# Graph layer on one Trainium2 core: masks made by GpSimd and turned by DMA, lower sums behind the projection, late one-hots at full width in two buffers

## The reference

```python
h    = max(layernorm(x), 0)                       # per node, over 128 features
idx  = the first 25 neighbours of each row of adj # in the order of their numbers
agg  = max over those of h[idx]                   # and with 0 where a row has <= 25 neighbours
out  = x + relu(concat([h, agg]) @ W + b)
```

## Time and profile before

| what | us |
|---|---|
| median of 3 runs | 698.95 (697.47 to 699.57) |
| the profiled execution | 697.45, its span 695.7 |
| PE busy in the span | 630.9 (91%) |
| DVE busy | 613.7 (88%) |
| ScalarE busy | 472.3 (68%) |
| POOL busy | 50.3 (7%) |
| DVE maxima of the picks (224) and of the late rounds (84) | 270.5 and 102.4 |
| ScalarE: masks (56) and copies of turned masks (64) | 57.4 and 62.2 |

### The profile page before, as it was taken

The page is one execution under the profiler, slowest core; times in us unless marked ns, Lnnn a source line. Parts: engine busy times, 40 slices in busy tenths (PEclk is TensorE's granted clock), DMA queues, the critical chain, the costliest instruction groups (busy, mean ns, idle before and its releaser), DMA issues.

```text
span 695.7 us, 10819 instructions
## 1 busy us (share of the span) xinstructions
PE 630.9 (91%) x3376; PEld 297.4 (43%) x3376; DVE 613.7 (88%) x813; ACT 472.3 (68%) x642; POOL 50.3 (7%) x41
## 2 busy tenths in 40 slices
PE   2479998999989999899999999899999999999976
PEld 2133443535445354443545344353535335353423
DVE  3368999899998999989998899989998899988997
ACT  2689478783777639775795947777497927959120
POOL 1300021000210002100030002100021000300000
PEclk9899999999999999999999999999999999999999
DMA  9520141510415103251303313151122411020100
GB/s 361 199 87 27 60 152 68 182 70 16 152 73 200 60 15 136 83 188 60 128 23 122 151 60 151 68 196 57 41 122 87 185 60 32 16 107 1 60 15 16
DMA packets 19127, 67.64 MB, mean 97 GB/s; under 512 B 4499, under 2 KB 7830, under 8 KB 16534
## 3 DMA queue, kind: packets, MB, share of 16 engines
q1 hardware_dynamic: 19094, 67.26, 25.7%
HBM read 42.08 MB, written 4.19 MB: 67 GB/s over the span
## 4 chain that ended last, share of the span: by engine, by line
PE 66%; DVE 16%; issue 10%; ACT 4%; DVEq 1%; DMA 1%; POOL 1%; ACTq 0%
PE picked L506 18%; PE picked L507 17%; PE ring L455 14%; DVE late_hot L684 4%; PE side L469 4%; PE ring L449 4%; DVE hot L659 4%; PE side L463 4%; DVE best L775 3%; DVE best L678 3%; PE final L534 2%; PE final L538 2%; PE final L491 1%; DMA adj_in<-in_adj_dram 1%; DVEq L771 1%
## 5 line engine op out<-in xcount | busy, mean ns | idle before, releaser
L678 DVE TENSOR_TENSOR best<-picked,best 128x1024 f32<-128x1024 f32 x224 | 270.5, 1218 | 38.2 <-PE picked L507 36.0
L506 PE MATMUL picked<-hot,h_hi 128*128 128x512 f16 x512 | 194.5, 380 | 15.0 <-DVE best L775 7.5
L507 PE MATMUL picked<-hot,h_lo 128*128 128x512 f16 x512 | 194.0, 379 | 0.0
L506 PE MATMUL picked<-late_hot,hi_skew 128*128 128x512 f16 x336 | 127.6, 380 | 13.1 <-DVE late_hot L684 8.2
L507 PE MATMUL picked<-late_hot,lo_skew 128*128 128x512 f16 x336 | 127.3, 379 | 0.0
L344 ACT ACTIVATE late_rank<-ring,late_bias 128x512 bf16<-128x512 f32 x128 | 81.4, 690 | 57.6 <-PE ring L455 57.6
L775 DVE TENSOR_TENSOR best<-picked,best 128x1024 f32<-128x1024 f32 x84 | 102.4, 1219 | 8.3 <-PE picked L507 8.2
L378 ACT COPY best<-picked 128x1024 f32<-128x1024 f32 x32 | 32.2, 1013 | 102.6 <-PE picked L507 102.6
L659 DVE TENSOR_SCALAR hot<-rank 128x4096 f16<-128x4096 bf16 x64 | 89.4, 1399 | 12.0 <-ACT rank L344 12.0
L349 ACT ACTIVATE past<-side,bias_cut 128x512 bf16<-128x512 f32 x128 | 88.3, 690 | 6.2 <-PE side L469 4.9
L344 ACT ACTIVATE rank<-ring,bias_big 128x512 bf16<-128x512 f32 x128 | 83.1, 692 | 5.2 <-PE ring L455 4.9
(11 more groups left out here) (76 smaller groups left out, 562.1 us busy)
## 6 DMA issues: line engine op xcount, KB each, us to landing
adj_in<-in_adj_dram SPq DMA_DIRECT2D x16, 2048.0 KB, 7.7
late_skew<-late SPq DMA_DIRECT2D x32, 192.0 KB, 2.3
x_in<-in_x_dram SPq DMA_DIRECT2D x8, 512.0 KB, 8.5
xres<-in_x_dram SPq DMA_DIRECT2D x16, 256.0 KB, 7.8
late_skew<-late SPq DMA_DIRECT2D x16, 256.0 KB, 2.4
late_skew<-late SPq DMA_DIRECT2D x32, 128.0 KB, 2.0
out_dram<-xres SPq DMA_DIRECT2D x16, 256.0 KB, 2.0
late_skew<-late SPq DMA_DIRECT2D x32, 64.0 KB, 1.9
```

Source lines behind the costliest of these rows:

```text
L506: nc.tensor.matmul(dst, hi[:, slot, k, :], onehot, start=start, stop=False)
L507: return nc.tensor.matmul(dst, lo[:, slot, k, :], onehot, start=False, stop=stop)
L678: nc.vector.tensor_tensor(best[:, half, s, :, :], picked[s][:, :, :], best[:, half, s, :, :], ALU.max).then_inc(picked_read, 1)
```

## The change

- Masks: in the prologue DVE makes group 0's from four separate loads of its adjacency, after the features' statistics; all others are made by POOL, from a strided view, into a layout ordered by class. SP turns each quarter with a transposing DMA into one of two buffers `mask_t[:, slot]`. ScalarE's masks and copies and PE's transposes are gone, and with them four of the twenty ring entries a step.
- The features are loaded ahead of the adjacency.
- The lower sums of g+2 stand at the end of step g, behind the projection; before, those of g+1 stood after use 4.
- Late ranks are spread over uses 4 to 9 (5 to 8 before), prefixes over 4 to 11 (5 to 12), ranks over 9 to 14 (9 to 13); the count follows use 11, not 9.
- Late one-hots are made at full width, into two of now four buffers of `hot`, in turn. The first is made after use 12.

```diff
-    LATE_WITH, PREFIX_WITH, RANK_WITH = spread_over(5, 8), spread_over(5, 12), spread_over(9, 13)
-    LATE_HOT_USES, COUNT_USE, MASK_USES = (10, 11), 9, (4, 9)
+    LATE_WITH, PREFIX_WITH, RANK_WITH = spread_over(4, 9), spread_over(4, 11), spread_over(9, 14)
+    LATE_HOT_USE, COUNT_USE = 12, 11
...
-        mask_t = sb("mask_t", [P, K, ROWS], BF16)
+        mask_t = sb("mask_t", [P, 2, K, ROWS], BF16)
...
-        hot = sb("hot", [P, 3, K, ROWS], F16)
-        late_hot = sb("late_hot", [P, K, ROWS], F16)
+        hot = sb("hot", [P, 4, K, ROWS], F16)
...
         # SP
-            load_adj(0, 0)
+            def turn_masks(slot):
+                sp.reg_add(masks_due, masks_due, Q)
+                for q in range(Q):
+                    sp.wait_ge(mask_made, q + 1)
+                    if q == 0:
+                        sp.wait_ge(mask_made, masks_due)
+                    sp.dma_start_transpose(mask_t[:, slot, :, q * P:(q + 1) * P],
+                                           mask[:, q, :, :].rearrange("p k j -> p (k j)")).then_inc(mask_turned, 16)
...
             load_x(0)
+            for q in range(Q):
+                sp.dma_start(adj_in[:, 0, q * N:(q + 1) * N], adj_v[0][:, q * N:(q + 1) * N]).then_inc(adj_first[q], 16)
             load_adj(1, 1)
...
             for g in (0, 1):
-                sp.wait_ge(mask_made, Q * (g + 1))
+                turn_masks(g)
                 load_adj(g + 2, g)
...
                     load_x(batch_of(it, u) + 1)
+                if not at_end(it, u, 2):
+                    turn_masks(u % 2)
                 if not at_end(it, u, 1):
                     skew_late(g + 1)
...
         # POOL
+            def make_masks(slot):
+                pool.reg_add(turned_due, turned_due, TURNED)
+                pool.reg_add(adj_due[slot], adj_due[slot], 16)
+                pool.wait_ge(mask_turned, TURNED)
+                pool.wait_ge(mask_turned, turned_due)
+                pool.wait_ge(adj_loaded[slot], adj_due[slot])
+                for q in range(Q):
+                    nc.gpsimd.tensor_scalar(mask[:, q, :, :], adj_in[:, slot, q * N:(q + 1) * N].rearrange("p (j k) -> p k j", k=K),
+                                            0.0, 0.0, ALU.is_equal, ALU.is_equal).then_inc(mask_made, 1)
...
             normalize(0)
             low_part(0, 0)
+            make_masks(1)
             def step(it, u):
                 g = g_of(it, u)
+                if not at_end(it, u, 2):
+                    make_masks(u % 2)
...
         # PE
+            def late_hot_of(turn, k):
+                return hot[:, bass.ds(1 + turn, 1), k, :]
...
                     pick_pair(g, use, slot)
-                    if use == PAIRS and more:
-                        lower_sums(at - TURNS)
...
                 with pe.Fori(0, n) as r:
+                    turn = nc.s_assert_within(r % 2, 0, 1, ...)
+                    pe.wait_ge(late_hot_made, done + (r + (g + 1)))
                     for s in range(2):
                         pe.wait_ge(picked_read, (g + 1) * READ - 1 + s)
-                        pe.wait_ge(late_hot_made[s], done + (r + (g + 1)))
                         pe.wait_ge(late_read[s], done + r + 1)
...
-                                last = pick(picked[s][:, j, :], hi_skew, lo_skew, k, late_hot[:, k, :], slot, i == 0, i == LINK - 1)
+                                last = pick(picked[s][:, j, :], hi_skew, lo_skew, k, late_hot_of(turn, k), slot, i == 0, i == LINK - 1)
...
-                if not at_end(it, u, 2):
-                    turn_mask(g + 2, at + TURN_AT, 0)
                 if more:
                     pick_pair(g + 1, 2, next_slot)
-                if not at_end(it, u, 2):
-                    turn_mask(g + 2, at + TURN_AT, 1)
-                if more:
-                    pick_pair(g + 1, 3, next_slot)
-                if not at_end(it, u, 2):
-                    turn_mask(g + 2, at + TURN_AT, 2)
-                    turn_mask(g + 2, at + TURN_AT, 3)
-                project(g, it, u, new_batch)
+                    pick_pair(g + 1, 3, next_slot)
+                project(g, it, u, new_batch)
+                if not at_end(it, u, 2):
+                    lower_sums(g + 2, u % 2)
...
         # DVE
+            def first_mask(q):
+                dve.wait_ge(adj_first[q], 16)
+                nc.vector.tensor_scalar(mask[:, q, :, :], adj_in[:, 0, q * N:(q + 1) * N].rearrange("p (j k) -> p k j", k=K),
+                                        0.0, None, ALU.not_equal).then_inc(mask_made, 1)
...
-            for q in range(Q):
-                make_mask(q, 0, 16, None)
             stats_of(0, range(K))
             moments_of(0)
+            first_mask(0)
+            make_gain(0)
+            for q in range(1, Q):
+                first_mask(q)
...
                 with dve.Fori(0, n) as r:
+                    turn = nc.s_assert_within((r + 1) % 2, 0, 1, ...)
                     for i in range(2):
                         dve.wait_ge(late_written[i], done + r + 1)
                         nc.vector.tensor_tensor(best[:, s, i, :, :], picked[i][:, :, :], best[:, s, i, :, :],
                                                 ALU.max).then_inc(late_read[i], 1)
-                        make_late_hot(i, numbers[:, bass.ds(r + 2, 1)])
+                        if i == 0:
+                            make_late_hot(bass.ds(1 + turn, 1), numbers[:, bass.ds(r + 2, 1)])
```

More of the change, by code:

```diff
@@ L405, in step @@
                 for use in range(PAIRS, USES):
-                    if use in MASK_USES and not at_end(it, u, 2):
-                        make_mask(MASK_USES.index(use), u % 2, 16 * (it * (UNROLL // 2) + u // 2 + 2), at)
                     for k in LATE_WITH[use]:
@@ L441, in take @@
                     pe.wait_ge(ring_read, at - 1)
-            def turn_mask(g, at, n):
-                if n == 0:
-                    pe.wait_ge(mask_made, Q * (g + 1))
-                take(at + n)
-                for j in range(2):
-                    for q in range(Q):
-                        last = nc.tensor.transpose(ring16[n % 2][:, j, q * P:(q + 1) * P], mask[:, q, 2 * n + j::K], eye[:, :])
-                last.then_inc(ring_written, 1)
             def accumulate(at, k, terms):
@@ L559, in _ @@
                 pick_pair(0, use, 0)
-            for n in range(TURNS):
-                turn_mask(1, FIRST_RING - TURNS, n)
+            lower_sums(1, 1)
             pe.wait_ge(h_turned, 2)
```

107 lines of the change are left out of this document (42 added, 65 removed).

## The result

The changed kernel takes 778.2 us (775.0 to 779.1, four runs), the kernel before 698.2 beside it (697.5 to 699.6): a ratio of 1.1135, 95% interval 1.1097 to 1.1173. The forecast was 722, with a range of 694 to 752. The sign was right, the size was not: 56 us are missing from the sum.

The account below looks back on a forecast made before the run. PE was taken to pace the steady stretch and a ring of waits between PE and DVE the late rounds. 697.45 - 18 + 20 + 22 - 1 = 720.4, with 1.5 for the median 722 us; range 694 to 752.

Parts of the forecast that it names:

- B: Late rounds: the full-width late one-hot lengthens each of 42 turns by 0.47 us, to 4.4; register address free; +20 us.
- A: Steady stretch (picks 4 to 15): transposes gone and lower sums moved shorten PE's work; -18 us, ends -8 and -28.
- C: POOL's masks hold DVE's one-hots and folds through a shared port in even and odd steps; +22 us, ends 0 and +60.
- D: Prologue: past ranks start near 26, late ranks where they did before; -1 us, ends -5 and +12.
- rival 4: POOL's masks are long, 3.2 us, and every burst meets DVE's work; 760 us, chance 0.09.
- Rival 3: DMA turning takes over 20 us a group, delaying POOL's masks, the skew and the prologue; 745 us, chance 0.12.
- Rival 2: DVE always has room, so A pays in full and POOL's masks cost nothing; 690 us, faster; chance 0.14.

Follow-up runs that it names:

- c_old: Changed kernel with later masks on ScalarE, group 1's on VectorE, half-width late one-hots in one buffer, and TensorE's order of before; 686.4 us (0.9819).
- c_half: Changed kernel with later masks on ScalarE, group 1's on VectorE, and half-width late one-hots in one buffer; 715.6 us (1.0233).
- c_full: Changed kernel with later masks on ScalarE where it idles and group 1's on VectorE, full-width late one-hots kept; 742.7 us (1.0625).
- b_ahead: Kernel before with full-width late one-hots in two alternating buffers, the next one issued ahead of both late maxima; 711.4 us (1.0170).
- a_half: Changed kernel with late one-hots as before (halves, one buffer), POOL still making the masks; 779.1 us (1.1172).
- a_old: Changed kernel with TensorE's order of before, full-width late one-hots and POOL's masks kept; 752.4 us (1.0755).
- c_ahead: Changed kernel with later masks on ScalarE, group 1's on VectorE, and the full-width late one-hot issued ahead of both late maxima; 716.5 us (1.0249).
- b_plain: Kernel before with 14 bursts of four spare POOL masks that nobody waits for, read one after another; 707.8 us (1.0130).
- a_contig: Changed kernel with POOL's masks reading the adjacency one after another and writing with a stride; 880.2 us (1.2570).

## Why the prediction missed, by its own steps

The kernels form a ladder, each one edit from the next. From the profiled runs, us:

| | to first fold | first to last fold | whole span |
|---|---|---|---|
| before | 82.6 | 606.7 | 695.7 |
| `c_old`: transposes out, DMA turning | 84.2 | 592.7 | 684.9 |
| `c_half`: and the new order | 87.2 | 618.9 | 714.5 |
| `c_full`: and edit B | 87.8 | 645.6 | 739.8 |
| after: and POOL's masks | 102.3 | 667.5 | 776.1 |

**A, forecast -18: measured 592.7 - 606.7 = -14 for taking the transposes out, and +26 for the rest of the same edit, +12 in all. This step failed most, by 30 us.** The transposes were rightly priced: from fold to fold an odd group's step is 38.0 us in `c_old` against 39.2 (0.9 forecast, 1.2 measured), an even one's with three rounds 39.6 against 41.3 (1.6 forecast, 1.7 measured); only the steps of groups 4, 8 and 12, where the unrolled loop starts again or ends, gain nothing. What failed is "the gain shows in the steady stretch, whose PE work falls from 20.82 to 19.1": it counted PE's work in the stretch and DVE's, and set the one against the other, but never laid the uses out one by one under the new spreads. The largest single piece is DVE's count and late one-hots two uses later (13.7 us): DVE is then late at the loop, where PE waits 0.93 us for it instead of 0.43. Next is the block of over 2 us of other matmuls behind use 9: DVE has two buffers of picks, and with its count gone from there it waits 1.80 us, however low the average is. The prediction listed these new places nowhere as a cost, and no rival had them. Its end of -8 named the two banks handed to and fro, but only as half of a gain lost, not as a loss of 12.

**B, forecast +20: measured +27 in the clean ladder, +39 alone on the kernel before.** The mechanism was right, including that the second buffer frees nothing behind the maximum (`b_ahead` shows it). The term was mis-sized: the turn forecast at 4.4 measured 4.65 to 4.81, since the one-hot grew by 0.54 and not 0.47, and the register address, taken at 0 with an end of 0.3 a round, costs 0.2 to 0.3, some 10 us in all. 42 x (4.65 - 3.95) = 29 is close to the 27; on the kernel before, 6 of the 39 are PE's pause where the loop starts again.

**C, forecast +22: measured 667.5 - 645.6 = +22 between the folds, by two errors that cancel.** A mask was taken at 2.0 us, at most 3.2; it takes some 4.7 undisturbed and 5.0 on average, beyond the upper end. But the sum priced the time in which a mask keeps DVE out, and that is 1.8 us at its start, close to the 2.0 (and 0.8 near its end for what begins there). A burst is then spread over 19 us with 4 x 1.8 = 7 of them in the way, not packed into 8; in the bursts read here it meets one to three of DVE's one-hots, folds or `agg_t` (366.56; then 415.21, 424.19 and 428.80). Both bursts of a pair of steps start near the late rounds (361.21, 412.82, 450.75); for the odd step that was forecast, for the even one 13 us into the steady stretch was. That the sum came out at +22 is luck in one more way: it holds only beside the full-width one-hot. With half-width one-hots the same masks cost 665.9 - 618.9 = 47 between the folds (`a_half` against `c_half`), and on the kernel before 60, the price of rival 4. The Trainium skill ("GPSIMD Engine Reference", "Performance pitfalls for Q7 kernels") led to an estimated 2.5 us a mask; this trace says 4.6 to 5.0, and the measurement decides.

**D, forecast -1: measured +20, the second failure.** The past ranks came where they were forecast (26.6). The late ranks were put "where they started before (51.16)" without asking what SP's queue holds ahead of the skew of `late`: the masks of group 1, on a slow engine. It is the wait that the prologue's queue order made; 14.5 of the 20 go when POOL's masks go (102.3 to 87.8), 3 with the new order, 1.6 are the turning's own.

Together: (12 + 18) + (27 - 20) + 0 + (20 + 1) = 58, and the miss of the spans is 80.4 - 23 = 57.

Rival 3 (a slow turning) fell: 1 MB was turned in 7.5 us, as D took it, where the Trainium skill ("Advanced Engine Details and Errata", section "X-Bar Transpose (TRN2)") had led to 3. Rival 2 was half right: without the transposes DVE does keep up, in the order of before.

What stays open: the last 9.5 us of the new order; PE's pause where the loop starts again in the kernels with parts of edit B alone; and the granted clock, which is 0.976 over the span in the changed kernel and in `a_old`, 0.993 before and 0.991 in `c_old`. In the changed kernel it is 0.79 of full from 38 to 78 us, where PE waits for the late ranks, and 0.96 in the steps from 333.58 and 422.93, so a part of each term is the lower level (1.2 GHz) and not waiting; that was not separated.

## What to carry to other kernels

A step with two engines at 90% is decided use by use: lay out what each instruction of the pacing engine stands between, and how many buffers cover it, before crediting a removal; `c_old` keeps the removal, drops the new order, the wide one-hots and POOL's masks, and is 1.8% faster than before. When a producer moves to another engine, ask what it holds there (a port, and for how long) and which in-order queue now waits for it, the first time round too. A second buffer issued behind the instruction that the reader's progress waits for gave nothing here, and issued ahead of it only made the width free (`c_ahead` 716.5, `c_half` 715.6). And when one run's excess is put down to one wait, add that wait up over the steps and see whether the steps agree: here two of fifteen had a pause of their own.

## What the runs showed of the hardware that was not expected

- A POOL instruction can keep DVE out for parts of its length only. With a strided read a mask of 4.6 us does so for its first 1.8 to 1.9 us and again for 0.8 near its end; contiguous, no hold is over 0.83 (`b_plain`); with a strided write one is 4.5 of 8.3 us (`a_contig`, 375.81). A one-hot of DVE that falls in the rest is not held.
- DVE keeps POOL out as well: a mask that begins while a one-hot is running takes 5.6 us instead of 4.6 (177.67).
- A POOL comparison of 128x1024 int32 into bf16 takes 3.6 us contiguous (4.1 with DVE in its way), 4.6 to 5.0 with the read 32 bytes apart, and 8.7 with the write strided instead; ScalarE's of the same strided shape takes 2.07.
- A matmul whose moving operand has its address from a register starts 0.30 to 0.46 us after the one-hot it waits for, one with a fixed address 0.13; the fifteen behind it follow at the usual 0.22.
- Turning 128x1024 bf16 by DMA takes some 1.35 us of SP's queue each. Behind a 2 MB load the first two of four take 3.0 to 5.1 us each in most steps (10.3 us for the four at 391.23). It makes small packets: 72131 under 512 B in the run, 4499 before.
